# A recurrent two-tower network: the path tower runs one step less ahead, with new orders on TensorE, ScalarE and VectorE

## The reference

```python
def _tower(x, w_in, b_in, blocks):
    h = _leaky(x @ w_in + b_in)
    for w1, b1, w2, b2 in blocks:
        h = _leaky(_leaky(h @ w1 + b1) @ w2 + b2 + h)
    return h

def step(prev_delta, xk):
    fk, k = xk
    d = jnp.where(k == 0, fk[:, DELTA_IDX], jax.lax.stop_gradient(prev_delta))
    fk = fk.at[:, DELTA_IDX].set(d)
    fe = _tower(fk[:, :N_FLAT], fw_in, fb_in, flat_blocks)
    pe = _tower(fk[:, N_FLAT:], pw_in, pb_in, path_blocks)
    h = _leaky(jnp.concatenate([fe, pe], axis=-1) @ cw1 + cb1)
    delta = jax.nn.sigmoid(h @ cw2 + cb2)[:, 0]
    return (delta, delta)
```

## Time and profile before

| | us |
|---|---|
| median of 3 runs | 1250.41 |
| lowest and highest run | 1250.08, 1253.89 |
| the profiled execution, its own time | 1254.54 |
| its span | 1252.7 |
| PE busy, PEld busy | 1247.0 (100%), 1063.5 (85%) |
| ACT busy, DVE busy | 931.0 (74%), 890.9 (71%) |

### The profile page before, as it was taken

How to read it: one execution, slowest core, us unless ns; L and a number is a source line. 1 busy time by engine, 2 the same in 40 slices (tenths; PEclk the granted TensorE clock), 3 DMA queues, 4 the chain that set the end, 5 groups by cost and what they waited for, 6 DMA issues and landing times.

```text
span 1252.7 us, 19624 instructions
## 1 busy us (share of the span) xinstructions
PE 1247.0 (100%) x6028; PEld 1063.5 (85%) x6028; DVE 890.9 (71%) x1950; ACT 931.0 (74%) x2049; POOL 11.8 (1%) x28
## 2 busy tenths in 40 slices
PE   9999999999999999999999999999999999999998
PEld 6888888888888888888888888888888888888886
DVE  3777777767777777777777777777777777777775
ACT  3777777777777777777777777777777777777776
POOL 1000000000000000000000000000000000000000
PEclk9999999999999999999999999999999999999999
DMA  2000000000000000001000000000000000000000
GB/s 75 30 10 31 13 10 30 13 30 10 24 20 11 29 13 24 17 10 33 11 23 19 12 30 10 30 13 11 29 14 29 10 21 22 11 23 12 13 4 1
DMA packets 14881, 24.50 MB, mean 20 GB/s; under 512 B 1983, under 2 KB 8214, under 8 KB 14782
## 3 DMA queue, kind: packets, MB, share of 16 engines
q1 hardware_dynamic: 13982, 22.33, 5.5%
q10 hardware_dynamic: 720, 0.66, 0.2%
q0 software_dynamic: 80, 0.26, 0.1%
HBM read 16.67 MB, written 6.55 MB: 19 GB/s over the span
## 4 chain that ended last, share of the span: by engine, by line
PE 98%; DMA 0%; ACT 0%; DVE 0%; issue 0%; ACTq 0%; DVEq 0%
PE ps_path L540 36%; PE ps_flat L540 18%; PE ps_res L543 18%; PE ps_head L670 9%; PE ps_head L665 9%; PE ps_head L683 2%; PE ps_head L678 2%; PE ps_path L570 2%; PE ps_flat L627 2%; DMA cb_col<-cb 0%; PE ps_path L565 0%; DVE f_t L448 0%; ACT delta L313 0%; DVE head_lo L482 0%; PE ps_flat L622 0%
## 5 line engine op out<-in xcount | busy, mean ns | idle before, releaser
L256 ACT ACTIVATE f_mid<-ps_flat,columns_sb 128x256 f32<-128x256 f32 x512 | 242.6, 474 | 161.9 <-PE ps_flat L540 155.5
L543 PE MATMUL ps_res<-f_mid,hidden_w 128*128 128x256 f32 x1024 | 306.1, 381 | 0.2
L540 PE MATMUL ps_path<-p_mid,hidden_w 128*128 128x256 f32 x1024 | 304.5, 380 | 0.0
L256 ACT ACTIVATE f_res<-ps_res 128x256 f32<-128x256 f32 x512 | 196.1, 384 | 62.4 <-PE ps_res L543 62.4
L540 PEld LDWEIGHTS ps_path<-p_mid,hidden_w 128*128 128x128 f32 x1024 | 190.9, 190 | 31.1 <-ACT p_mid L256 0.2
L543 PEld LDWEIGHTS ps_res<-f_mid,hidden_w 128*128 128x128 f32 x1024 | 168.6, 189 | 55.4 <-ACT f_mid L256 1.8
L414 DVE SCALAR_TENSOR_TENSOR p_sum<-ps_path,columns_sb,p_in 128x512 f32<-128x512 f32 x128 | 96.1, 751 | 126.9 <-PE ps_path L540 126.9
L256 ACT ACTIVATE p_mid<-ps_path,columns_sb 128x512 f32<-128x512 f32 x256 | 176.1, 688 | 6.4 <-PE ps_path L540 6.4
L476 DVE CAST head_hi<-head 128x256 fp32r<-128x256 f32 x256 | 75.3, 294 | 128.8 <-ACT head L256 128.7
L448 DVE SCALAR_TENSOR_TENSOR f_t<-delta,columns_sb,ps_flat 128x256 f32<-128x256 f32 x256 | 123.1, 481 | 50.0 <-ACT delta L313 48.9
L256 ACT ACTIVATE head<-ps_head,cb_scaled 128x256 f32<-128x256 f32 x256 | 121.2, 474 | 45.7 <-PE ps_head L670 39.6
(11 more groups left out here) (49 smaller groups left out, 1454.9 us busy)
## 6 DMA issues: line engine op xcount, KB each, us to landing
x_in<-x_hi SPq DMA_DIRECT2D x127, 48.0 KB
x_in<-x_lo SPq DMA_DIRECT2D x127, 48.0 KB
chunk_x<-x SPq DMA_DIRECT2D x16, 192.0 KB, 2.4
x_hi<-chunk_hi SPq DMA_DIRECT2D x16, 192.0 KB, 1.9
x_lo<-chunk_lo SPq DMA_DIRECT2D x16, 192.0 KB, 2.0
out<-delta SPq DMA_DIRECT2D x128, 2.0 KB
hidden_w<-hidden ACTq DMA_DIRECT2D x1, 384.0 KB, 5.7
hidden_w<-hidden ACTq DMA_DIRECT2D x1, 256.0 KB, 3.0
```

Of the source, the lines that this page charges most:

```text
L256: return act.activation(dst, src, ACT.Prelu, bias=bias, alpha=NEG)
L540: return pe.matmul(dst, weight[w_name], src, start=True, stop=True)
L543: return pe.matmul(dst, weight[w_name], src, start=False, stop=True, skip_group_check=True)
```

## The change

The path tower's operations move by one step: where the bodies held `path_in(k + 3)`, `path_1a(k + 3)`, `path_1b(k + 2)`, `path_2a(k + 2)`, `path_2b(k + 1)`, they now hold `path_in(k + 2)`, `path_1a(k + 2)`, `path_1b(k + 1)`, `path_2a(k + 1)`, and on DVE `path_2b(k)` (on PE `path_2b` of `k + 1` ends one body instead of reaching into the next). No operation changes its engine, its operands or its waits. The orders within the bodies of PE, ACT and DVE are new, and so are the three openings. The lists of SP and POOL are unchanged.

```diff
@@ ACT body
-                path_1b(k + 2)
+                path_1b(k + 1)
                 flat_2b(k, 0)
                 head_out(k, 1)
+                path_in(k + 2)
                 head_out(k, 0)
-                path_in(k + 3)
+                path_2a(k + 1)
                 delta_out(k, 1)
-                path_2a(k + 2)
                 delta_out(k, 0)
-                path_1a(k + 3)
+                path_1a(k + 2)
@@ DVE body
                 flat_1b_old(k, 0)
-                path_1b_sum(k + 2)
+                path_2b_sum(k)
+                path_2b(k)
                 flat_2b_old(k, 1)
+                path_1b_sum(k + 1)
                 flat_2b_old(k, 0)
-                path_2b_sum(k + 1)
-                path_2b(k + 1)
@@ DVE opening
-            split_first_chunk()
-            split_input_weights()
             flat_delta(0, 0)
             flat_in(0, 0)
+            split_input_weights()
+            flat_1b_old(0, 0)
             flat_delta(0, 1)
-            flat_1b_old(0, 0)
             flat_in(0, 1)
+            split_first_chunk()
...
             path_2b_sum(0)
             path_2b(0)
             split_chunk(1)
-            path_1b_sum(2)
+            path_1b_sum(1)
             head_high(0, 1)
@@ PE body
                 flat_1b(k, 1)
-                path_1b(k + 2, 1)
+                path_1b(k + 1, 1)
                 flat_1b(k, 0)
                 flat_2a(k, 1)
-                path_2b(k + 1, 1)
+                combine_path(k, 0)
                 flat_2a(k, 0)
                 flat_2b(k, 1)
-                combine_path(k, 0)
+                path_in(k + 2)
+                combine_path(k, 1)
                 flat_2b(k, 0)
                 combine_flat(k, 1)
+                path_2a(k + 1, 0)
+                combine_flat(k, 0)
+                path_2a(k + 1, 1)
+                output_high(k, 1)
+                path_1a(k + 2, 0)
+                output_low(k, 1)
+                flat_x(k + 1, 1)
+                output_high(k, 0)
+                path_1a(k + 2, 1)
+                output_low(k, 0)
                 flat_x(k + 1, 0)
...
+                path_2b(k + 1, 0)
+                path_2b(k + 1, 1)
                 flat_1a(k + 1, 1)
-                path_1b(k + 3, 0)
+                path_1b(k + 2, 0)
```

## The result

The changed kernel takes **1261.74 us** (median of four runs, 1261.46 to 1262.64), against 1252.15 for the kernel before in the same comparison (1250.08, 1250.41, 1253.89, 1253.97). The ratio is 1.0077, 95% interval 1.006 to 1.0095: slower, as forecast, but by more, and just outside the forecast range of 1250.0 to 1261.0. The four times of the kernel before lie at two levels, near 1250.3 and near 1253.9, and the median falls between them; against the lower one the changed kernel is 0.9% slower (1261.74 to 1250.25). The profiled execution of the changed kernel took 1261.9 us, so here the profiler adds nothing.

A forecast was written before the change was run, and what follows sets the result against it. PE's own work was taken to bound the steady state, 126 bodies of 9.58 us. Opening -0.15, steady +3.3 and end +0.3 made +3.5 us: 1253.9 on the median, 1258.0 on the profiled execution, weighted to 1256.6 us, range 1250.0 to 1261.0.

The forecast's parts named there:

- PE's own work: PE's matmuls in the steady body: same 27 operations, 9.58 to 9.60 us a step, +0.01, between -0.02 and +0.02.
- DVE's place of path_2b: Steady body: combine_path(k, 0) waits for a p_res2 made in the same body; round 9.61 against 9.58 us, +3.3 us in all.
- The round over `combine_path`: Steady loop from output_low(k, 1) over DVE's path_2b to combine_path and back: 4.95 + 4.66 = 9.61 us.
- the one over f_in: Steady loop over f_in to flat_1a(k + 1, 1): 1.93 us of latency plus 7.68 of PE work, again 9.61 us.
- The opening: Before body 1: the wait for chunk 1 eats 3.7 us of saved path work; -0.15 us, from -3.7 to +1.
- rival 1: Opening: PE's clock falls to half in the wait ahead of path_in(2), 3 us added, 1259.6 us; chance 0.17.
- The idle is interrupted soon: Opening: argument given against PE's clock falling to half during the wait ahead of path_in(2), a gap of about 3 us.
- The tail: Last three steps: the path work moved out of the opening fills PE's gaps there, +0.3 us, from 0 to +0.5.
- The base: Kernel before: profiled 1254.54 against median 1250.41 us; profiler or earlier clock rise, the second held twice as likely, two thirds of 4.1 added.
- Rival 2: Opening: POOL's cast of chunk 1 starts before 25 us, path_in(2) doesn't wait, 3.7 us won, 1250.3 us; chance 0.12.
- Rival 3: Steady loop: one of nine terms is shorter by 0.03, PE's own work rules, 0 to +1 us, 1253.3; chance 0.16.
- Rival 4: Steady loop: small DVE delays such as chunk splits show, 0.02 us per step, 2.5 us added, 1259.1; chance 0.10.

The follow-up runs named there:

- f_in round cut: Changed kernel with flat_delta(k, 1) reading, from step 2 on, the delta of two steps before instead of the last one; 1255.13 us.
- late split: DVE's split_chunk(1) moved behind head_low(0, 0) in the opening: in the kernel before 1250.64 us, in the changed kernel 1257.24 us.
- path_2b rounds cut: Changed kernel with combine_path(k, g) reading the p_res2 of the step before and waiting only for its copy; 1261.71 us.

## Why the prediction was right or wrong

The direction was right, and so were the two kinds of cost: a round of dependences now longer than PE's own work, and a wait for chunk 1 that eats what the shorter opening saves. The step that failed is the steady term, "DVE's place of path_2b", put at +3.3 us by a round of 9.61 us and measured at +6.5 by a step that grew by 0.0515. The round over `combine_path` to which it gave the wait costs nothing; the one over f_in sets the step, and its sum left out the second wait of `flat_1b(k, 1)`, 0.025 us a step. Against the profiled execution the whole sum gave 1258.0, and 1261.9 was measured: 3.9 us, of which 3.2 lie in the steady step and 0.8 in the opening, with 0.1 back in the tail. Another 1.4 went by the choice of the base.

**PE's own work: right.** Predicted 9.58 to 9.60, with 0.02 either way; with the f_in round cut it is 9.573.

**The round: mis-sized, and the wrong one named first.** Predicted 9.61 and +3.3 us, measured 9.633 and, with the means of 9.636 and 9.584, 126 x 0.0515 = +6.5. The prediction had two rounds of 9.61 and put the one over `combine_path(k, 0)` first. Cutting that round changed nothing, cutting the other gave everything. Its latency part was right (1.93 predicted; 1.92 to 1.93 in the trace). Its PE part was short: 17 pairs at 0.4316 are 7.34 and not 7.33, `path_in` costs 0.236 and not 0.23, and the larger part, the 0.025 at `flat_1b(k, 1)`, wasn't in the sum at all. That makes 9.64, with every term read to 0.01. `flat_1b(k, 1)` waits for two engines, ACT's f_mid and DVE's `flat_1b_old(k, 1)`, which end within 0.01 us of each other. Without that second wait the step is 9.608, which is the predicted 9.61; what exactly of the second wait costs the 0.025 stays open. The prediction had said that the round was known to 0.03, from 0 to +6.9 us; the truth lay at that upper end, and the central value did not lean there although every term left out could only lengthen the round.

**The opening: the chain was right, its end was rival 1.** Predicted and measured: chunk 0 split at 11.39, 11.04; the cast at 28.33, 27.56; `path_in(2)` not before 30.25, 29.37; body 1 at 35.95, 36.77. Up to the cast the terms were 0.77 us too long: 0.35 nearly all because in_raw had been there earlier (DVE's cast of it starts at 8.19, not 8.51), 0.42 because chunk 1 took 6.86 from issue to cast instead of 7.28. From the end of the cast on the prediction had 7.12 us at full clock. With the clock kept up it is 7.15, with the fallen clock 8.71. So rival 1 happened, at 1.6 us instead of the 3 it was priced at: the fall came 1.6 us behind the start of `path_in(2)` and lasted 3.4 us, not 6 (in other traces 6.8). The gap ahead of `path_in(2)` was 1.47 us, half of what was predicted, and a second one of 0.32 us and a thin stretch followed: PE was busy for 1.31 of the 3 us around them. The prediction had called a gap of 3 us a borderline case by the Trainium skill, page TensorE: Matmul & The Clock Gate, section on HAM oscillation, which lets an idle gap take the clock back from some length on. A gap of 1.47 us is short of the one that the section speaks of, so by its rule this gap would not have taken the clock; the trace shows that it went, and the measurement decides. "The idle is interrupted soon" was no argument against a fall.

**The tail: right**, +0.24 us for a predicted +0.3.

**The base: half seen.** The prediction named the two possible reasons of the 4.1 us between the profiled execution and the median of before, and it held the right one for twice as likely: the clock rises sooner in the lower runs, and the changed kernel doesn't profit. The traces at 1254.54 (before) and 1249.91 (before with the late split) show the first, body 1 at 36.10 and 31.36. The changed kernel shows the second: the traces with a rise near 15 us (f_in and path_2b rounds cut, 15.4) start body 1 at 38.08 and 35.95, around 36.77. But then it mixed the two bases, 1253.9 + 2/3 x 4.1, and a mixture is a time at which neither case lies. The likelier one alone would have given 1258.0.

**The other rivals.** Rival 2 (no wait for chunk 1) was false as the kernel stands. Its price was nearly right when it was made true: -3.7 predicted against the kernel before, 32.79 - 36.10 = -3.31 measured with the late split, with a clock that rose 0.54 us later. Rival 3 (slack in the loop) was false. Rival 4 (+0.02 per step by more slips) has about the right size, but not its cause: all but three of the steady steps are within 0.02 of 9.633, those with a chunk split too.

**What the change is worth without its opening.** With rises of the clock at 24.02 and 23.48 body 1 starts at 32.79 in the changed kernel with the late split and at 36.10 in the kernel before, 3.3 us sooner. Between the earliest of either kind it is 1.7 us sooner (29.63 against 31.36), although there the clock rose 2.7 us later in the changed one (16.07 against 13.35). The steady part costs 6.7 us more. One step less of lead is a gain of some three microseconds once, for a loss of 0.05 us in every step.

## What to carry to other kernels

Where PE is busy without a gap, the waits of its matmuls show nothing; look at those of its weight loads (127 for f_in here, 3 before), compare the period of one operation over ten steps, and look for pairs that last 0.61 to 0.63 where the others last 0.59. When a round comes out within 1% of the bounding engine's own work, count every wait of every matmul on it, the second ones too, and lean to the long side. An opening that waits for a transfer hides where the clock rises, so compare executions of the two kernels with the rise at the same place, or take the opening off the span first.

## What was not expected of the hardware

- The clock rose at 13.35 us in one execution and at 23.48 in another, with the same order of work up to there; the executions are 4.6 us apart. In four traces it rose at 4.1 to 4.5 us, fell at 7.5 to 7.9 and rose again at 14.3 to 14.7, and in a fifth it rose at 5.0, fell at 11.8 and rose again at 22.1.
- A stretch in which TensorE was busy for 1.31 of 3 us, with no single idle piece above 1.47 us, was followed by 3.4 us at half clock.
- The same 192 KB load took 4.5 us from its issue to the cast with four loads of x ahead of it, and 6.9 with ten.
- With the second of two waits that end together taken off one matmul, its weight load followed the other by 0.06 us instead of 0.10, and a step was 0.025 us shorter.
